# Upsampling matmuls of a resampling kernel on two tiles of 64 rows by 128 columns instead of four of 64 by 64

## What is computed

```python
out = input + bias[None, :, None, None]
upf = up_filter * UP
out = _sep_upfirdn(out, upf, UP, 1, UP_PAD)               # both axes upsampled by 2
out = jax.nn.leaky_relu(out, NEG_SLOPE) * FLRELU_SCALE
out = _sep_upfirdn(out, down_filter, 1, DOWN, DOWN_PAD)   # both axes decimated by 2
```

## Time and profile before

| | |
|---|---|
| time, median of 3 runs | 7656.16 us (7654.64 to 7658.82) |
| the profiled execution: its time | 7660.9 us |
| the profiled execution: its span | 7658.7 us |
| TensorE, matmuls busy | 7119.1 us, 93% |
| TensorE, weight loads busy | 6407.7 us, 84% |
| VectorE busy | 5921.4 us, 77% |
| ScalarE busy | 4596.5 us, 60% |
| GpSimd busy | 2518.8 us, 33% |

### The profile page before, as it was taken

The page is one execution under the profiler, slowest core; times in us unless marked ns, Lnnn a source line. Parts: engine busy times, 40 slices in busy tenths (PEclk is TensorE's granted clock), DMA queues, the critical chain, the costliest instruction groups (busy, mean ns, idle before and its releaser), DMA issues.

```text
span 7658.7 us, 691127 instructions
## 1 busy us (share of the span) xinstructions
PE 7119.1 (93%) x302021; PEld 6407.7 (84%) x302021; DVE 5921.4 (77%) x11619; ACT 4596.5 (60%) x9070; POOL 2518.8 (33%) x3076
## 2 busy tenths in 40 slices
PE   7999967029999999999999999999999999999999
PEld 3444442029999999999999999999999999999998
DVE  8999950877777777777777777777777777777776
ACT  0000002337777777777777777777777777777776
POOL 0000000014444444444444444444444444444443
PEclk9999978569999999999999999999999999999999
DMA  7777724003333333333333333333333333333332
GB/s 303 316 310 308 310 118 183 3 24 96 96 96 96 96 96 96 96 96 96 96 96 96 96 96 96 96 96 96 96 96 95 96 96 96 96 96 96 96 96 80
DMA packets 1261531, 925.62 MB, mean 121 GB/s; under 512 B 183504, under 2 KB 1233104, under 8 KB 1242576
## 3 DMA queue, kind: packets, MB, share of 16 engines
q1 hardware_dynamic: 1252112, 890.13, 36.2%
q10 hardware_dynamic: 9344, 34.61, 1.7%
HBM read 621.50 MB, written 303.04 MB: 121 GB/s over the span
## 4 chain that ended last, share of the span: by engine, by line
PE 78%; issue 0%; DVE 0%; DMA 0%; ACT 0%; SPq 0%; POOL 0%; DVEq 0%
PE bank L1009 26%; PE bank L1004 24%; PE twin L1004 13%; PE twin L1009 13%; PE twin L1139 2%; DVE x_sum L1237 0%; DMA img<-in_x 0%; DVE leaky L1213 0%; DMA low<-conv_dram 0%; SPq L915 0%; ACT dn L1204 0%; ACT slope_t L1173 0%; POOL img L963 0%; DVE up L1222 0%; SPq L916 0%
## 5 line engine op out<-in xcount | busy, mean ns | idle before, releaser
L1213 DVE SCALAR_TENSOR_TENSOR leaky<-bank,slope_t 128x512 f32<-128x512 f32 x4096 | 2636.5, 685 | 1034.9 <-ACT slope_t L1173 1034.9
L1004 PE MATMUL bank<-up_t,up 64*64 64x133 f32 x65536 | 2760.3, 276 | 7.1 <-issue 6.3
L1009 PEld LDWEIGHTS bank<-down_t,leaky 64*64 64x64 f32 x131072 | 2235.9, 135 | 101.8 <-issue 92.9
L1009 PE MATMUL bank<-down_t,leaky 64*64 64x35 f32 (+1 forms) x131072 | 2306.3, 222 | 10.0 <-issue 8.0
L1173 ACT ACTIVATE slope_t<-bank 128x512 f32<-128x512 f32 x4096 | 2225.6, 599 | 7.9 <-PE bank L1004 7.9
L1004 PEld LDWEIGHTS bank<-up_t,up 64*64 64x64 f32 x65536 | 2041.1, 133 | 9.5 <-issue 9.5
L972 POOL TENSOR_TENSOR low_d<-low_v 128x252 f32<-128x252 f32 x512 | 310.9, 607 | 5038.9 <-ACT low_v L1195 5038.9
L1189 ACT ACTIVATE res<-twin 128x512 f32<-128x512 f32 x1024 | 611.6, 597 | 1447.7 <-PE twin L1009 1447.7
L1237 DVE SCALAR_TENSOR_TENSOR x_sum<-lift,coef,img 128x128 f32<-128x128 f32 x4096 | 1428.9, 409 | 11.7 <-POOL img L963 11.7
L1004 PE MATMUL twin<-up_t,x_sum 64*64 64x133 f32 x32768 | 1386.5, 278 | 9.2 <-DVE x_sum L1237 5.3
L1009 PE MATMUL twin<-down_t,dn 64*64 64x35 f32 (+1 forms) x65536 | 1358.8, 221 | 6.0 <-issue 5.7
(11 more groups left out here) (154 smaller groups left out, 2154.7 us busy)
## 6 DMA issues: line engine op xcount, KB each, us to landing
img<-in_x SPq DMA_DIRECT2D x1024, 256.0 KB, 2.9
out<-res SPq DMA_DIRECT2D x1024, 256.0 KB, 2.2
rows_in<-in_x SPq DMA_DIRECT2D x48, 4224.0 KB, 14.0
rows_in<-in_x SPq DMA_DIRECT2D x16, 4096.0 KB, 13.8
conv_dram<-conv ACTq DMA_DIRECT2D x64, 512.0 KB, 4.2
xb<-conv_dram SPq DMA_DIRECT2D x8, 4096.0 KB, 13.2
low<-conv_dram SPq DMA_DIRECT2D x1024, 32.0 KB, 2.2
xx<-conv_dram SPq DMA_DIRECT2D x2, 2048.0 KB, 10.3
```

Source lines behind the costliest of these rows:

```text
L1004: return pe.matmul(acc[cols(c), a:b], src[cols(rt), cols(c)], up_t[cols(rt), a:b], start=first, stop=False, skip_group_check=True)
L1009: return pe.matmul(acc[cols(c), a:b], src[cols(rt)], down_t[cols(rt), k, a:b], start=first, stop=False, skip_group_check=True)
L1213: v.scalar_tensor_tensor(out=leaky[1 - m % 2][:, e, i].rearrange("p k w -> p (k w)"), in0=u2_acc[e][i][:], scalar=GAIN, in1=slope_t[e][i][ ...
```

## The change

`up()` loses its parameter `c`. Its stationary operand is now the data of 64 rows and all 128 columns, its output all 128 partitions, and the loops over `c` in `first_up` and `second_up` go. `down()` and the bilinear pass stay as they are.

```diff
-                    def up(acc, src, rt, c, first):
+                    def up(acc, src, rt, first):
 
                         a, b = ((0, UP_REACH), (UH - UP_REACH, UH))[rt]
-                        return pe.matmul(acc[cols(c), a:b], src[cols(rt), cols(c)], up_t[cols(rt), a:b],
+                        return pe.matmul(acc[:, a:b], src[cols(rt)], up_t[cols(rt), a:b],
                                          start=first, stop=False, skip_group_check=True)
                     def first_up(p, half):
                         for e in range(2):
-                            for c in range(2):
-                                for rt in range(2):
-                                    i = rt ^ half
-                                    mm = up(u1_acc[i][:, e * UH:(e + 1) * UH], x_sum[p][:, e, i, :], rt, c, half == e == 0)
+                            for rt in range(2):
+                                i = rt ^ half
+                                mm = up(u1_acc[i][:, e * UH:(e + 1) * UH], x_sum[p][:, e, i, :], rt, half == e == 0)
                         return mm
                     def second_up(p, e, half):
                         for k in range(2):
-                            for c in range(2):
-                                for rt in range(2):
-                                    i = rt ^ half
-                                    mm = up(u2_acc[e][i][:, k * UW:(k + 1) * UW], up1[p][:, i, e, k * P:(k + 1) * P], rt, c, half == k == 0)
+                            for rt in range(2):
+                                i = rt ^ half
+                                mm = up(u2_acc[e][i][:, k * UW:(k + 1) * UW], up1[p][:, i, e, k * P:(k + 1) * P], rt, half == k == 0)
                         return mm
```

## The result

| | before | changed |
|---|---|---|
| time, median of four runs | 7655.4 us (7654.1 to 7658.82) | 8554.01 us (8551.61 to 8556.42) |
| ratio to before | | 1.1173 (1.1154 to 1.1192) |
| span of the profiled execution | 7658.7 us | 8549.4 us |
| instructions | 691127 | 592823 |

The change makes the kernel 12% slower. The forecast was 7803; the rival by which a switch of tile shape empties the array said 8490. The time lies within the stated range, and the likeliest case was the wrong one.

What follows compares the result with a forecast made beforehand. TensorE was taken to set the pace. Longer load, waiting halves and fewer instructions, 134 + 42 - 32 = +144 ns a step, times 1024 steps, gave +147 us and 7803 us; range over all cases 7640 to 8700, the forecast's own 7700 to 7900.

Steps and rivals of the forecast that it cites:

- the rival by which a switch of tile shape empties the array: At six shape changes a step, loads wait until the array is empty: 189 + 6x ns on top of 144; 8490 us; chance 0.38.
- Streaming: no change: An upsampling group still takes four rounds of 133 columns, 4 x 113.3 ns, and the longer load hides behind such matmuls.
- The longer load, +134 ns: First load of an upsampling behind a decimation lies open: 53.4 ns at 2.5 places a step; bounds 0 and 336.
- The waiting halves, +42 ns: A wide upsampling waits for the later column half: 14 ns at three places a step; bounds 0 and 150.
- Fewer instructions, -32 ns: 16 instructions fewer a group give back 64 ns at the branch, every second step; bounds 0 and 75 a step.
- x: Passage time through the array at each shape switch in the rival of the emptied array: between 0 and 160 ns, middle 80.
- The chased load: Rival: matmuls use columns already loaded, so the longer load costs nothing: +10 ns a step, 7666 us; chance 0.12.
- the lighter queue: Rival: with half the upsampling instructions the sequencer stays ahead and recovers half of 179 ns where groups meet: 7564 us; chance 0.08.

Runs made afterwards that it cites:

- the unrolled one: The kernel before with TensorE's loop unrolled over four steps instead of two, nothing else changed: 12153 us, 1.587.
- 72 columns instead of 128: The changed kernel, but in the hardware loop its upsampling matmuls load and compute 72 of the 128 columns: 8408 us, 1.0979 to the kernel before.
- the kernel with everything wide: The changed kernel with decimations and the bilinear pass on two tiles of 64x128 too, so one tile shape in the loop: 12811 us, 1.6728 to the kernel before.
- The run without switches: The kernel before, all tiles 64x64, but in the hardware loop the upsamplings compute only the lower 64 output partitions, on two tiles: 7610 us, 0.9938.
- six, eight, four and two switches: Six: the change itself. Wide 64x128 in the others: eight, only second upsampling, 8997 us; four, only first, 8313, or single groups, 8341; two, run of four groups, 7882.
- the tiles of 128 rows: The changed kernel with its loop's upsamplings on two tiles of 128 rows by 64 columns, same number of switches: 8400 us, 1.0968 to the kernel before.

## Why the prediction was wrong

**The bound** was read rightly: TensorE sets the time in all runs, in the unrolled one together with its fetches, and ACT and DVE stay busy for under 80% of the loop. One share in its account of a step is off: half of the bilinear pass's 0.25 us is 125 ns and not 110, so 164 ns and not 179 lie where groups meet. No term of the forecast goes by that.

**Streaming: no change** held. In the changed kernel the groups of a run start every 0.45 us (4009.51, 4009.97, 4010.42), and a load of 187 ns hides behind a matmul of 133 columns, as the matmuls of L480 suggested for a load of as many columns. They were weaker evidence than they looked, since most of their loads have shorter records:

```profile
L480 PEld LDWEIGHTS bank<-cst,xs x38: 139/141/195, 1070.4 to 1074.5; 128*128 128x128 f32 x38
```

**The longer load, +134 ns** had the right mechanism: 0.05 us at a place, as the kernel with everything wide shows without a switch. 72 columns instead of 128 gave back 143 ns a step; by the 47 ns a place that is three places. The forecast's 2.5 places were short by the bilinear pass: in the changed kernel it covers no load, since a switch follows it.

**The waiting halves, +42 ns** can't be told apart in any run; in the changed kernel a switch stands where they would wait. The term was also worked out wrongly: at 58 ns for four loads two places are 29 ns and not 14, so by its own rows it should have been 3 x 29 = 87, and the forecast about 7850.

**Fewer instructions, -32 ns** had the right sign. The run without switches gained 47 ns, inside the bounds of 0 and 75, of which about 27 are left for the sequencer by the estimate given there. In the changed kernel nothing of it shows apart: at the branch the switch's pause covers the sequencer's.

**The step that failed** is the one between the sum and the forecast. The sum took in only what rows of before could price, and the one thing that they could not price, two shapes back to back, was put at zero. The runs showed in its place six switches a step, each with about 90 ns in which nothing streams or loads and with a load in the open behind it, and a step longer by 878 ns. The switch was named as a rival with 0.38 against 0.42. The rival's mechanism holds, and 90 ns is inside its bounds of 0 and 160 for x. The middle, 80, was taken for want of a row, and gave 8490 instead of 8554. That 144 + 189 + 6 x 90 = 873 comes so near the measured 870 is in part luck: no run shows the 42 ns in it, and the working had no cover at the branch, where 0.60 us fell to 0.55. The sentence "nothing in the trace speaks for or against it" was true, and should have moved the forecast to the case that six new events a step are not free, the more so as a stated rule was on that side: the Trainium skill, "TensorEngine Tiling (Array Packing)", Key Properties, has it that changing the tiling mode drains TensorE, and the runs agree, with six, eight, four and two switches.

**The chased load** and **the lighter queue** are refuted as causes that decide: the first by the group of 0.54 us after a decimation in the kernel with everything wide, the second by its size, at most 47 ns against 870.

What is shown is a pause at each change of shape and its size. That the array empties during it is the likely reading, since it counts from the end of the streaming (0.20 us after the start of a matmul of 133 columns, 0.15 after one of 35), but no record shows the array itself. Every switch here also leads to a tile that takes in parts of tiles still in use. Whether a new shape on a free part of the array would wait as well, no run tests, and all the matmuls are float32.

## What to carry to other kernels

Keep one tile shape on TensorE within a loop, or order the work so that long runs share a shape: count the switches, not the matmuls. Per switch a step got longer by 160 to 167 ns in the runs with four and eight switches, by 146 with six, and by 109 where the branch and a slow place covered part of both. With loads as short as before it was 121 (the tiles of 128 rows). That is as much as the streaming of a round of four tiles, or more. Choose the shape by the group with the shortest matmuls, since its pace goes by the load, and that one doubled with the columns (58 to 112 ns a round). And where a trace lacks a new kind of event that happens thousands of times, don't let its price be zero in the likeliest case.

## What the runs showed of the hardware

- Switching between 64x64 and 64x128, or 64x64 and 128x64, holds the next load back until about 90 ns after the last streaming ended, and nothing of the new shape is loaded ahead. To 64x128 it cost 218 ns a step for two switches (each partly covered), 639 and 666 for four, 878 for six, 1306 for eight; to 128x64, 727 for six.
- With all tiles 64x128 and short decimation matmuls behind loads of 128 columns, the clock swung between full and half, 0.75 on average, though matmul and load records covered all but a few ns in 10 us. What it is about this stream that the clock responds to is open.
- With a loop body of TensorE of two steps the whole execution fetched 0.52 MB on the instruction queue; with one of four steps it fetched 46 MB and ran 59% longer.
